# Second layer's cross-attention: float32 scores of 16 rows in TensorE's four row groups, in place of stacked bf16 parts

## The chip, the cores and the metric

The kernel runs on one core of a Trainium2 chip. The core has TensorE (matmuls), VectorE, ScalarE, GpSimd and queues for transfers. TensorE reads its operands from SBUF (128 partitions) and writes to PSUM, eight banks of 128 partitions x 512 float32. The metric is the device time of one execution in microseconds (us). The kernel before takes 3047.73 us (median of three runs, 3041.04 to 3049.35).

## What is computed

A decoder of two layers on x of shape (4, 512, 256): layer one has a state-space block, an attention with a feed-forward, a cross-attention and eight experts; layer two has an attention in blocks of 64, a cross-attention, and sixteen experts with a shared feed-forward. The change is in layer two's cross-attention alone:

```python
def _L1_xattn_ref(Q, K, V, Wq, bq, Wk, bk, Wv, bv, We, be):
    B, L, D = Q.shape            # 4, 512, 256
    H, E = 16, D // 16           # 16 heads of 16
    q = (Q @ Wq + bq).reshape(B, L, H, E)
    k = (K @ Wk + bk).reshape(B, S, H, E)
    v = (V @ Wv + bv).reshape(B, S, H, E)
    scores = jnp.einsum('blhe,bshe->bhls', q, k)
    A = jax.nn.softmax(scale * scores, axis=-1)      # scale = 1/4
    out = jnp.einsum('bhls,bshd->blhd', A, v).reshape(B, L, H * E)
    return out @ We + be
x = x + _L1_xattn_ref(_layernorm(x), ctx, ctx, ...)
```

## The kernel before

Each engine has one program, written out by hand, and they meet at semaphores. `Sig` names a semaphore with its count per sample. `Lane` is a ring of PSUM banks: `fill` makes TensorE wait until the tile that had the bank is drained, `take` makes the reader wait until the tile is full. In layer two `LBA` (banks 0, 1) is drained by ScalarE and `LBV` (banks 2, 3) by VectorE. `LBM` is one bank (1) for ten tiles of the softmax ("md": rows of maxima `MT_AT`, flips `FL_AT`, flips back `OTB_AT`), `LBO` one bank (0) for the weighted sums.

Layer two runs sample by sample (`for b in range(B)`, four samples). Activations have features on partitions and 512 positions along the free axis. One sample is, in TensorE's order:

1. Rotary query and key tiles (`rope_pair`), values (`v2_`), then the cross-attention's keys (`yk`, two tiles, drained by ScalarE to `kf`). Query and key rows of the block attention are rearranged by 16 transfers on SP's queue (L580).
2. The block attention (`block_scores`, `transpose_weights`, `weigh_blocks`), with the shared feed-forward of the sample before put in between (`ffn_gate`, `ffn_out`; none in sample 0). VectorE masks, finds maxima and sums, and in between splits `kf` into three bf16 parts (`split_step`, five steps, L2215 casts and L2217 subtractions).
3. The output projection (`wo`), whose sum with x VectorE makes; then the layer norm: mean (`norm_mean`), `centre` on VectorE, squares on ScalarE, `norm_var`, root, reciprocal, `norm_rows`, `norm_apply`. Between these stand the key stacks (`stack`, L1168): for each head three bf16 matmuls with 0/1 matrices (`sel_k`) put the parts, in the order `K_ORDER`, on 128 partitions, and ScalarE (L1723) drains them to `k_stack`. A product of two stacks is the sum of eight products of parts, near float32.
4. Queries (`yq`) from the normed x, values (`yv`); VectorE adds the bias, scales by 0.25 (L2257) and splits the queries (five steps); then sixteen query stacks.
5. Scores for the maxima (`scores_for_max(u)`, L1208): 64 tiles of 128 queries x 512 keys, one bf16 matmul each; VectorE takes the negated maximum of every row (`row_max`, L2272). The first sixteen use banks 4 to 7, later ones banks 2 and 3. Per group of four heads VectorE splits the maxima in three bf16 parts (`split_max`, L2285, L2287), TensorE turns them to rows (`rows_of_max`, L1216), VectorE casts these (`take_rows`, L2293).
6. The loop over 32 steps v (`scores_less_max(v)`): two heads and 128 keys to a step, transposed scores of 512 queries in banks 4+5 or 6+7, two bf16 matmuls (L1227) and two of 3 rows that add the negated maximum (L1230). ScalarE takes the exponential of both banks at once (L1750). Every second step `weigh_heads` (L1240) multiplies with values and a column of ones for four heads, in four column groups of 32. In step v TensorE issues the scores of step v + 1 first, then the maxima of a later group (`MAX_PER`, two or three a step), then a flip, rows or weighing if due.
7. Flips of the sums, division, flip back, the projection `we`, and the norms for the next sample and for the experts.

After four samples come the router and the sixteen experts, which the change does not touch. While layer one's experts run, VectorE sets up the selection matrices, and ScalarE's queue loads layer two's weights (`w1_loads`).

Of the kernel before, what the change touches and what calls it, by code (L numbers as in the profile page):

```python
# [7 lines left out]
P = 128  # L8
# [14 lines left out]
Q_ORDER, K_ORDER = (0, 0, 1, 1, 0, 2, 1, 2), (0, 1, 0, 1, 2, 0, 2, 1)  # L23
SR = len(Q_ORDER) * LE


# [10 lines left out]
MAX_PER = [3, 3] + [2] * 19  # L37
KS_PARTS = (0, 4, 8, 12, 14, 16)
# [33 lines left out]
class Lane:  # L72
# [22 lines left out]
    def take(self, eng, rnd, group, i):  # L95

        j = self.upto(group, i)
        eng.wait_ge(self.full.sem, self.full.at(j + 1, rnd))
        return self.banks[j % len(self.banks)]


def decoder_program(nc, A, out):
# [5 lines left out]
    with ctx:  # L108
# [127 lines left out]
        w_yq, w_yk, w_yv, w_ye, b_yv = take(KD, D), take(KD, D), take(KD, D), take(KD, D), take(D)  # L236
# [4 lines left out]
        sel_q, sel_k = [[take16(8, SR) for _ in range(3)] for _ in range(2)]  # L241
# [31 lines left out]
        kf, k_parts = take(KD, L), [take16(KD, L) for _ in range(3)]  # L273
        v1o = take(NC * LH * 2 * LE).rearrange("p (c h e) -> p c h e", c=NC, h=LH)
        pr1 = [take(2, L) for _ in range(4)]
        xnn1 = pr1[0].rearrange("p a b -> p (a b)").rearrange("p (c n) -> p c n", c=NC)
        negm1, nm_parts, nm_rows = take(NC, LH), take16(NC, P), [take16(L) for _ in range(2)]
        o_sb, rinv1 = [take(L) for _ in range(2)], take(NC, 4)
        nm_cols = nm_parts.rearrange("p c (h i) -> p c h i", i=32)
        outn, sd0, x_odd = take(NC, D), take(NC), take(KD, L)  # L280

        qf = take(KD, L, at=blocks_at)
        q_parts = [take16(KD, L, at=blocks_at + (2 + i) * L) for i in range(3)]
        xc0, sq0 = take(KD, L, at=blocks_at), take(KD, L, at=blocks_at + 2 * L)
        q_stack = take16(LH, L, at=turns_at)
        k_stack, oTb, o_all = take16(LH, L, at=scores_at), take(KD, L, at=scores_at + 8 * L), take(NC, D, at=scores_at + 10 * L)
# [101 lines left out]
        s1_full, s1_max, p1_ready = sig("s1_full", U1), sig("s1_max", U1), sig("p1_ready", V1)  # L388
        s2_full, pv1_done, o1_step = sig("s2_full", V1), sig("pv1_done", 4 * (NC - 1)), sig("o1_step", 8)
        kq_step, nm_step, sel_made = sig("kq_step", 10), sig("nm_step", 20), sig("sel_made")  # L390
        def rounds(*groups):
# [3 lines left out]
                   rounds(("v2_", 2), ("yk", 2), ("pair", 3 * NC), ("ks", LH), ("qs", LH), ("xn", 2)))  # L395
        LBV = Lane(LV.full.later(B), LV.drained.later(B), bank[2:4],
                   [("rope_a0", 2), ("rope_b0", 6)] + [(f"{name}{b + i}", tiles) for b in range(B) for name, i, tiles in (
                       ("wo", 0, 2), ("yq", 0, 2), ("yv", 0, 2), ("we", 0, 2), ("rope_a", 1, 2), ("logit", 0, 1), ("rope_b", 1, 6)) if b + i < B])
# [4 lines left out]
        LBM = Lane(sig("md_tile"), sig("md_drained"), bank[1:2], (("md", 10),))  # L403
# [32 lines left out]
        def _(sp):  # L436
# [139 lines left out]
            for b in range(B):  # L576
# [9 lines left out]
                if b + 1 < B:  # L586
                    sp.wait_ge(LBV.full.sem, LBV.full.at(LBV.upto(f"yv{b}", 2)))
                    load_ctx(b + 1)
# [15 lines left out]
        def _(pe):  # L604
# [389 lines left out]
            pe.wait_ge(sel_made.sem, 1)  # L994
# [79 lines left out]
            for b in range(B):  # L1074
# [13 lines left out]
                for m in range(KD):  # L1088
                    project(LBA, f"yk{b}", m, w_yk, ctxB)
                w(qk_here, 16 * 16)  # L1090
                act_has(f"v2_{b}", 2)

# [72 lines left out]
                def stack(group, h, select, parts):  # L1165
                    t = LBA.fill(pe, 0, group, h)
                    for j in range(3):
                        r = mm(t[0:SR], select[j][:, h % 8, :], parts[j][:, h // 8, :], start=j == 0, stop=j == 2)  # L1168
                    r.then_inc(LBA.full.sem, 1)

                def key_stacks(n):
                    for h in range(KS_PARTS[n], KS_PARTS[n + 1]):
                        stack(f"ks{b}", h, sel_k, k_parts)

                w(kq_step, 5)
                key_stacks(0)
# [10 lines left out]
                for m in range(KD):  # L1187
                    project(LBV, f"yq{b}", m, w_yq, xn)
# [8 lines left out]
                def scores_for_max(u):  # L1197
# [6 lines left out]
                    else:  # L1204
                        if u >= 4 * NC + 2:
                            w(s1_max, u - 1)
# [1473 lines left out]
```

## Time and profile before

| | |
|---|---|
| runs (us) | 3047.73, 3041.04, 3049.35 |
| profiled execution | 3043.07 us, span 3041.3 us |
| mean granted TensorE clock | 0.936 |
| TensorE matmul, share of the span | 2707.5 us, 89% |
| TensorE weight load | 1579.5 us, 52% |
| VectorE | 1508.0 us, 50% |
| ScalarE | 1149.9 us, 38% |
| reductions for the maxima (L2272), 256 | 163.0 us, 685 ns each |
| exponentials (L1750), 128 | 129.3 us, 1024 ns each |
| drains of the stacks (L1723), 128 | 75.9 us, 596 ns each |
| layer two's four samples | from about 1741 to 2580 us |

A row of windows gives its bounds and length, then the busy us (with the number of instructions) of TensorE, its weight loads, VectorE, ScalarE and GpSimd, then the granted TensorE clock (1.00 is 2.4 GHz, 0.50 is 1.2 GHz), the share of DMA and GB/s. Busy time of TensorE is modelled from the starts of its matmuls; neighbouring records overlap, so lengths are best read from one start to the next. A float32 matmul leaves two records, a bf16 one leaves one. In the timelines a line merges consecutive instructions of one line of the code; in square brackets stands the idle time of the engine before it and what ended it. "PE" is TensorE, "PEld" its weight loads, "DVE" VectorE, "ACT" ScalarE.

### The profile page before, as it was taken

What the parts mean: (1) busy time and instruction counts of PE and PEld (TensorE: products, weight loads), DVE (VectorE), ACT (ScalarE), POOL (GpSimd) and SP (SyncE); (2) the same over time, 40 slices, a digit from 0 to 9 for tenths busy, and PEclk for the clock granted to TensorE, in tenths of its full rate; (3) what the DMA queues carried; (4) which work ended last, traced back from release to release, by engine and by line L of the source; (5) the groups of instructions that cost most, each with busy time, mean ns of one, the idle gap of its engine ahead of it and who ended that gap; (6) DMA issues with size and microseconds to landing.
All of it is one profiled execution on the core that took longest, in us unless ns stands there. A gap on an engine that the chain in (4) does not pass through costs nothing. (4 is left out here: it accounts for less than half of the span.)

```text
span 3041.3 us, 40614 instructions
## 1 busy us (share of the span) xinstructions
PE 2707.5 (89%) x16481; PEld 1579.5 (52%) x16481; DVE 1508.0 (50%) x2382; ACT 1149.9 (38%) x1989; POOL 681.7 (22%) x364
## 2 busy tenths in 40 slices
PE   7779999999999999999869888988988998699997
PEld 4355534753285426653358653452542533487776
DVE  5565356833784277634611146346455554644442
ACT  4673245533472255424313225345344344011111
POOL 0254035801572065503320200000000000022222
PEclk9889999999999999999879879999899898699999
DMA  5540003100120003000179610100100101144443
GB/s 191 217 157 22 1 0 113 38 1 1 49 101 2 1 1 129 22 1 0 41 269 333 247 25 7 22 22 1 22 22 1 22 8 52 50 146 149 146 166 84
DMA packets 62130, 218.76 MB, mean 72 GB/s; under 512 B 12293, under 2 KB 28122, under 8 KB 45178
## 3 DMA queue, kind: packets, MB, share of 16 engines
q1 hardware_dynamic: 45802, 187.39, 17.1%
q0 software_dynamic: 9568, 18.75, 2.5%
q10 hardware_dynamic: 6576, 10.05, 0.9%
q8 instruction: 130, 2.13, 0.3%
q14 instruction: 54, 0.44, 0.0%
HBM read 171.98 MB, written 39.99 MB: 70 GB/s over the span
## 5 line engine op out<-in xcount | busy, mean ns | idle before, releaser
L610 PE MATMUL psum<-arena 128*128 128x256 f32 (+7 forms) x4160 | 1084.1, 412 | 67.7 <-ACT arena L1488 11.5
L610 PEld LDWEIGHTS psum<-arena 128*128 128x128 f32 (+1 forms) x4160 | 679.6, 200 | 423.9 <-issue 312.4
L2500 POOL TENSOR_TENSOR arena<-arena 128x1024 f32<-128x1024 f32 x128 | 299.9, 2370 | 110.2 <-DVE arena L1958 95.2
L1958 DVE TENSOR_TENSOR_SCAN arena<-arena,psum 128x512 f32<-128x512 f32 x256 | 291.5, 1201 | 26.1 <-PE psum L751 17.7
L751 PEld LDWEIGHTS psum<-arena 128*128 128x128 f32 x2048 | 242.9, 198 | 47.5 <-ACT arena L1518 40.3
L751 PE MATMUL psum<-arena 128*128 128x128 f32 x2048 | 253.5, 283 | 1.9 <-issue 1.9
L2535 POOL DMA_INDIRECT arena<-xn,arena x32 | 31.6, 987 | 959.8 <-DVE arena L2442 908.4
L2507 POOL TENSOR_TENSOR arena<-arena 128x1024 f32<-128x1024 f32 x32 | 75.9, 2373 | 656.8 <-ACT arena L1606 656.8
L2272 DVE TENSOR_REDUCE arena<-psum 128x1 f32<-128x512 f32 x256 | 163.0, 685 | 84.5 <-PE psum L1208 84.3
L2052 DVE SCALAR_TENSOR_TENSOR arena<-psum,arena 128x1024 f32<-128x1024 f32 x128 | 156.9, 1244 | 80.4 <-PE psum L896 80.1
L1606 ACT ACTIVATE arena<-arena 128x1024 f32<-128x1024 f32 x128 | 146.7, 1146 | 110.1 <-DVE arena L2052 109.9
L1750 ACT ACTIVATE arena<-psum 128x1024 f32<-128x1024 f32 x128 | 129.3, 1024 | 115.9 <-PE psum L1230 115.4
L1790 ACT ACTIVATE arena<-psum 128x256 f32<-128x256 f32 x128 | 49.2, 384 | 320.3 <-PE psum L610 320.3
L1511 ACT ACTIVATE arena<-arena 128x512 f32<-128x512 f32 x256 | 162.9, 708 | 0.0
L2511 POOL TENSOR_TENSOR arena<-arena 128x1024 f32<-128x1024 f32 x64 | 151.2, 2363 | 10.2 <-ACT arena L1606 1.3
L907 PE MATMUL psum<-arena 128*64 128x512 f32 x512 | 138.2, 617 | 15.5 <-ACT arena L1606 7.4
L896 PE MATMUL psum<-arena 64*128 64x512 f32 x512 | 142.5, 638 | 2.7 <-ACT arena L1584 2.7
L2036 DVE RECIPROCAL arena<-arena 128x256 f32<-128x256 f32 x64 | 110.9, 1743 | 46.1 <-ACT arena L1598 46.1
L1405 PE MATMUL psum<-arena 128*128 128x256 f32 x512 | 116.0, 378 | 0.0
L1518 ACT ACTIVATE arena<-arena 128x128 f32<-128x128 f32 x256 | 81.5, 390 | 82.4 <-PE psum L751 60.2
L2465 DVE TENSOR_TENSOR arena<-arena,psum 128x256 f32<-128x256 f32 x128 | 53.3, 421 | 116.3 <-ACT arena L1790 114.5
L1723 ACT ACTIVATE arena<-psum 128x512 bf16<-128x512 f32 x128 | 75.9, 596 | 80.7 <-PE psum L1168 78.1
(299 smaller groups left out, 3217.4 us busy)
## 6 DMA issues: line engine op xcount, KB each, us to landing
arena<-in_W SPq DMA_DIRECT2D x46, 1024.0 KB
arena<-c_rows SPq DMA_DIRECT2D x32, 512.0 KB, 3.8
arena<-in_Wg SPq DMA_DIRECT2D x16, 1024.0 KB, 4.9
arena<-in_Wu SPq DMA_DIRECT2D x16, 1024.0 KB, 7.6
arena<-in_Wd SPq DMA_DIRECT2D x16, 1024.0 KB, 10.0
arena<-in_xT SPq DMA_DIRECT2D x8, 512.0 KB, 5.4
zs_all<-arena SPq DMA_DIRECT2D x4, 1024.0 KB, 3.9
ut_all<-arena SPq DMA_DIRECT2D x4, 1024.0 KB, 8.7
```

The costliest lines, as they stand in the source:

```text
L610: r = mm(dst, w, x, start=i == 0, stop=i == len(pairs) - 1)
L751: r = mm(bank[4 + c][:, q * P:(q + 1) * P], duT[:, q, c * P:(c + 1) * P], diag[n % 2][:, q, :], start=True, stop=True)
L896: i = mm(bank[2 + 2 * (u % SBUFS) + r], xkT[64 * r:64 * r + 64, hp, kc * P:(kc + 1) * P], xqT[64 * r:64 * r + 64, hp, :], start=True, stop ...
L907: i = mm(bank[0][64 * r:64 * r + 64, :], v1[:, kc, 2 * hp + r, :], t2[u % TBUFS][:, r, :], start=kc == 0, stop=kc == NC - 1)
L1511: A_(dA[n % 2][:, c, :], dl[:, c, :], ACT.Exp, scale=aneg[:, c, n:n + 1]).then_inc(dA_ready.sem, 1)
L1606: A_(t2[u % TBUFS], rl[u % RBUFS], ACT.Square, scale=0.125, bias=vec[:, V_NB:V_NB + 1])\
L1750: A_(pr1[v % 4], psum[:, 4 + 2 * (v % 2):6 + 2 * (v % 2), :], ACT.Exp).then_inc(p1_ready.sem, 1)
L1958: V.tensor_tensor_scan(hs[n % 3][:, c, :], dA[n % 2][:, c, :], bank[4 + c], 0.0, ALU.mult, ALU.add)\
L2052: V.scalar_tensor_tensor(rl[u % RBUFS], t, minus_nb8, bound[:, kc, :].unsqueeze(1).broadcast_to([P, 2, L]), ALU.max, ALU.min).then_inc(rel ...
L2272: V.reduce_max(negm1[:, qc, h:h + 1], t, AX.X, negate=True).then_inc(s1_max.sem, 1)
L2500: nc.gpsimd.tensor_tensor(h, h, c_all[:, n % CBUFS, :].unsqueeze(1).broadcast_to([P, 2, L]), ALU.mult)\
L2511: nc.gpsimd.tensor_tensor(t, t, t2[kc], ALU.add).then_inc(tsum_step.sem, 1)
```

## The change

Queries and keys keep float32, and no parts or stacks are made. `_lay_out` pads each head of 16 columns of Wq and Wk (and of the biases) to 32 with zeros, so that the projections give four tiles of four heads, head j of a tile on partitions 32j to 32j + 15; partition 32j + 16 is 0 in the queries (until the negated maximum is added) and 1 in the keys (a bias of 1). Scores for the maxima are one float32 matmul of 16 rows, the scores of the loop one of 17 rows, in row group j. The order of the maxima is by group of four heads, block of queries, head; so four consecutive ones lie in four row groups. The negated maxima stand in columns 32j + 16 of `row_neg`, are transposed in float32, and added to the queries (`add_rows`). The scale of 0.25 goes to the exponential. `Placed` replaces the ring for the maxima after the first sixteen, their rows, flips and flips back: banks 1, 2, 3 in turn as long as there are maxima, then bank 1. 24 maxima instead of 20 are done ahead of the loop. Values are projected where the old keys were (ahead of the block attention), the keys' four tiles stand between the steps of the norm. The load of the next context waits for the keys instead of the values.

```diff
@@ constants
-Q_ORDER, K_ORDER = (0, 0, 1, 1, 0, 2, 1, 2), (0, 1, 0, 1, 2, 0, 2, 1)
-MT_AT, FL_AT, OTB_AT = (0, 1, 3, 6), (2, 4, 7, 8), (5, 9)
-MAX_AHEAD = 20
+MAX_AHEAD = 24
+def _cross_tiles():
+    order = [("max", 16), ("max", 17), ("row", 0)] + [("max", u) for u in range(18, MAX_AHEAD)]
+    for v in range(32):
+        order += [("max", u) for u in range(MAX_AHEAD + 2 * v, min(MAX_AHEAD + 2 * v + 2, 64))]
+        if v % 8 == 3 and v > 8:
+            order.append(("flip", v // 8 - 1))
+        if v % 8 == 5 and v < 24:
+            order.append(("row", v // 8 + 1))
+        if v == 22:
+            order.append(("back", 0))
+    return order + [("flip", 3), ("back", 1)]
+class Placed:
+    def fill(self, pe, rnd, tile):
+        n = self.number[tile]
+        before = [i for i in range(n) if self.places[i] == self.places[n]]
+        if before:
+            pe.wait_ge(self.drained.sem, self.drained.at(before[-1] + 1, rnd))
+        return self.banks[self.places[n]]
...
+        LBM = Placed(sig("md_tile"), sig("md_drained"), bank, cross,
+                     [1 + i % 3 if i <= cross.index(("max", U1 - 1)) else 1 for i in range(len(cross))])
@@ TensorE
                 norm_mean(x_b, 4)
-                key_stacks(1)
+                for g in range(2):
+                    project(LBA, f"yk{b}", g, w_yk, ctxB)
                 norm_var(mid_norm(b), sq, 5)
-                key_stacks(2)
+                project(LBA, f"yk{b}", 2, w_yk, ctxB)
                 norm_rows(mid_norm(b), sd, 4)
-                key_stacks(3)
+                project(LBA, f"yk{b}", 3, w_yk, ctxB)
                 w0(nb.out, mid_norm(b) + 1)
-                for m in range(KD):
-                    project(LBV, f"yq{b}", m, w_yq, xn)
...
+                for g in range(2):
+                    project(LBA, f"yq{b}", g, w_yq, xn)
 
                 def scores_for_max(u):
...
-                    mm(t, q_stack[0:SR, h, qc * P:(qc + 1) * P], k_stack[0:SR, h, :],
-                       start=True, stop=True).then_inc(s1_full.sem, 1)
+                    mm(t, q4[32 * j:32 * j + LE, g, qc * P:(qc + 1) * P], k4[32 * j:32 * j + LE, g, :],
+                       start=True, stop=True).then_inc((s1_full if u < LH else LBM.full).sem, 1)
...
                 def scores_less_max(v):
...
                     for j in (j0, j0 + 1):
-                        mm(bank[4 + 2 * (v % 2) + j % 2], k_stack[0:SR, 4 * g + j, kc * P:(kc + 1) * P],
-                           q_stack[0:SR, 4 * g + j, :], start=True, stop=False)
-                    for j in (j0, j0 + 1):
-                        r = mm(bank[4 + 2 * (v % 2) + j % 2], ones16[32 * j:32 * j + 3, :],
-                               nm_rows[g % 2][32 * j:32 * j + 3, :], start=False, stop=True)
+                        r = mm(bank[4 + 2 * (v % 2) + j % 2], k4[32 * j:32 * j + LE + 1, g, kc * P:(kc + 1) * P],
+                               q4[32 * j:32 * j + LE + 1, g, :], start=True, stop=True)
                     r.then_inc(s2_full.sem, 1)
...
+                for qc in range(NC):
+                    if qc == 0:
+                        act_has(f"yq{b}", 1)
+                    if qc >= 2:
+                        project(LBA, f"yq{b}", qc, w_yq, xn)
+                    for u in range(NC * qc, NC * (qc + 1)):
                         scores_for_max(u)
...
@@ ScalarE
+                def keys_in(g):
+                    t = LBA.take(act, 0, f"yk{b}", g)
+                    A_(k4[:, g, :], t, ACT.Identity, bias=vec[:, V_BK + g:V_BK + g + 1]).then_inc(LBA.drained.sem, 1)
@@ VectorE
-                    split_step(0, kf, k_parts, p)
...
+                def add_rows(g):
+                    t = LBM.take(dve, b, ("row", g))
+                    V.tensor_tensor(q4[:, g, :], q4[:, g, :], t, ALU.add).then_inc(LBM.drained.sem, 1)
```

## Rows read from the trace of the kernel before

**Rows 1.** Windows of sample 1: busy us per engine, clock, DMA share, GB/s.

```profile
2053.00:2068.00 15.00, 13.59 (x61) 5.13 (x58) 12.64 (x24) 7.81 (x14) 0.00 (x0) 1.00 0.00 1
2068.00:2137.00 69.00, 61.34 (x334) 16.27 (x334) 36.63 (x72) 35.82 (x37) 0.00 (x0) 0.98 0.00 1
```

**Rows 2.** Timeline of sample 1, output projection to maxima: start, length, engine, line.

```profile
2021.98 3.60 PE L610 MATMUL psum<-arena 128*128 128x512 f32 x8
...
2025.62 0.69 DVE L2173 TENSOR_TENSOR arena<-arena,psum 128x512 f32<-128x512 f32 x1 [1.03 <-PE psum L610]
...
2028.23 1.88 PE L610 MATMUL psum<-arena 128*128 128x512 f32 x4
...
2033.94 1.84 PE L610 MATMUL psum<-arena 128*128 128x1 f32 x16
...
2038.45 1.05 PE L1022 MATMUL psum<-arena 128*128 128x128 f32 x8
...
2040.82 7.17 PE L610 MATMUL psum<-arena 128*128 128x512 f32 x24
...
2052.90 1.03 PE L1208 MATMUL psum<-arena 128*128 128x512 bf16 x4
2053.31 2.48 DVE L2272 TENSOR_REDUCE arena<-psum 128x1 f32<-128x512 f32 x4 [2.10 <-PE psum L1208]
```

**Rows 3.** Timeline, layer one's cross-attention: matmuls in two row groups.

```profile
411.82 2.85 PE L896 MATMUL psum<-arena 64*128 64x512 f32 x12 [0.69 <-ACT arena L1584]
```

**Rows 4.** Timeline of sample 1, the loop: a weighing, its successors; exponentials 21 and 31.

```profile
2077.92 1.07 PE L1240 MATMUL psum<-arena 128*32 128x512 f32 x8
2078.92 0.61 PE L1227 MATMUL psum<-arena 128*128 128x512 bf16 x2
...
2081.87 1.07 PE L1240 MATMUL psum<-arena 128*32 128x512 f32 x8
...
2117.28 1.02 ACT L1750 ACTIVATE arena<-psum 128x1024 f32<-128x1024 f32 x1 [2.07 <-PE psum L1230]
...
2134.38 1.02 ACT L1750 ACTIVATE arena<-psum 128x1024 f32<-128x1024 f32 x1 [1.11 <-PE psum L1230]
```

**Rows 5.** Timeline: waits at the block attention, and ahead of layer one's experts.

```profile
1546.77 0.69 PE L967 MATMUL psum<-arena 128*128 128x128 f32 x2 [31.20 <-DMA arena<-slots_x]
...
1973.48 0.78 PEld L1101 LDWEIGHTS psum<-arena 16*64 16x64 f32 x64 [0.76 <-DMA arena<-arena]
...
1986.19 0.90 PE L1101 MATMUL psum<-arena 16*64 16x64 f32 x64 [0.91 <-issue]
```

**Rows 6.** Timeline of sample 1, from maximum 15 to the first exponential.

```profile
2064.91 0.20 DVE L2285 CAST arena<-arena 128x16 bf16<-128x16 f32 x1
...
2067.48 0.68 DVE L2293 CAST arena<-psum 128x512 bf16<-128x512 f32 x1
...
2068.22 0.61 PE L1227 MATMUL psum<-arena 128*128 128x512 bf16 x2 [0.21 <-DVE arena L2293]
...
2069.23 1.28 ACT L1750 ACT_TABLE_LOAD   x1 [3.44 <-PE psum L1230]
...
2070.53 3.07 ACT L1750 ACTIVATE arena<-psum 128x1024 f32<-128x1024 f32 x3
```

**Rows 7.** Windows around a fall of the clock (columns as rows 1), and exponentials there.

```profile
2084.30:2087.70 3.40, 1.86 (x15) 0.56 (x16) 2.06 (x4) 1.19 (x2) 0.00 (x0) 1.00 0.00 0
2087.70:2091.10 3.40, 3.40 (x13) 0.36 (x6) 0.98 (x2) 1.23 (x3) 0.00 (x0) 0.50 0.00 0
...
2087.07 1.02 ACT L1750 ACTIVATE arena<-psum 128x1024 f32<-128x1024 f32 x1 [2.21 <-PE psum L1230]
...
2090.86 1.02 ACT L1750 ACTIVATE arena<-psum 128x1024 f32<-128x1024 f32 x1 [0.90 <-PE psum L1230]
...
2106.54 1.02 ACT L1750 ACTIVATE arena<-psum 128x1024 f32<-128x1024 f32 x1 [2.21 <-PE psum L1230]
...
2108.94 1.02 ACT L1750 ACTIVATE arena<-psum 128x1024 f32<-128x1024 f32 x1 [0.24 <-PE psum L1230]
```

More of the change, by code:

```diff
@@ L99, in take, with __init__, upto @@
         return self.banks[j % len(self.banks)]
+class Placed:
+    def __init__(self, full, drained, banks, tiles, places):
+        self.full, self.drained, self.banks, self.places = full, drained, banks, places
+        self.number = {tile: n for n, tile in enumerate(tiles)}
+        self.full.per = self.drained.per = len(tiles)
+    def upto(self, tile):
+        return self.number[tile] + 1
+    def fill(self, pe, rnd, tile):
[4 more added lines that the diff above has]
+        return self.banks[self.places[n]]
+    def take(self, eng, rnd, tile):
+        eng.wait_ge(self.full.sem, self.full.at(self.upto(tile), rnd))
+        return self.banks[self.places[self.number[tile]]]
 def decoder_program(nc, A, out):
@@ L1087, in _ @@
                 pe.wait_ge(ld_cB.sem, ld_cB.at(16, b))
-                for m in range(KD):
-                    project(LBA, f"yk{b}", m, w_yk, ctxB)
+                for i in range(2):
+                    t = LBV.fill(pe, 0, f"yv{b}", i)
+                    for c in range(2):
+                        r = acc(t[:, c * D:(c + 1) * D],
+                                [(ctxB[:, k, (2 * i + c) * P:(2 * i + c + 1) * P], w_yv[:, k, :]) for k in range(KD)])
+                    r.then_inc(LBV.full.sem, 1)
                 w(qk_here, 16 * 16)
                 act_has(f"v2_{b}", 2)
+                dve_has(f"yv{b}", 2)
                 def block_scores(p):
@@ L1163, in _ @@
                     project(LBV, f"wo{b}", m, w_wo1, oT1)
[L1165 to L1176, printed above, removed]
                 dve_has(f"wo{b}", 2)
@@ L1222, in scores_less_max @@
                     if v % 8 == 0:
-                        w(LBM.drained, MT_AT[g] + 1)
+                        w(LBM.drained, LBM.upto(("row", g)))
                     if v >= 2:
@@ L1276, in _ @@
                 scores_less_max(0)
-                n_max = MAX_AHEAD
                 for v in range(V1):
@@ L1294, in _ @@
                     turn_y(b + 1)
+                w(LBM.drained, LBM.upto(("max", U1 - 1)))
                 tiles = [LBV.fill(pe, 0, f"we{b}", m) for m in range(KD)]
@@ L1300, in _ @@
                         flip_back(1)
-                    w(LBM.drained, OTB_AT[k] + 1)
+                    w(LBM.drained, LBM.upto(("back", k)))
                     for m in range(KD):
@@ L1687, in _ @@
                     r.then_inc(LBA.drained.sem, 1)
-                for m in range(KD):
-                    t = LBA.take(act, 0, f"yk{b}", m)
-                    A_(kf[:, m, :], t, ACT.Identity, bias=vec[:, V_BK + m:V_BK + m + 1]).then_inc(LBA.drained.sem, 1)
                 def drain_pair(p):
@@ L1740, in drain_o @@
                     if g >= 2:
-                        w(LBM.full, FL_AT[g - 2] + 1)
+                        w(LBM.full, LBM.upto(("flip", g - 2)))
                     A_(o_sb[g % 2], t, ACT.Identity).then_inc(LBO.drained.sem, 1)
@@ L2208, in pair_out @@
                     r.then_inc(bo_step.sem, 1)
-                def split_step(base, v, parts, i):
-                    if i > 0:
-                        w(kq_step, base + i)
-                    if i % 2 == 0:
-                        V.tensor_copy(parts[i // 2], v).then_inc(kq_step.sem, 1)
-                    else:
-                        V.tensor_tensor(v, v, parts[i // 2], ALU.subtract).then_inc(kq_step.sem, 1)
+                for i in range(2):
+                    t = LBV.take(dve, 0, f"yv{b}", i)
+                    V.tensor_tensor(v1o[:, 2 * i:2 * i + 2, :, 0:LE],
+                                    b_yv.rearrange("p (h e) -> p h e", h=LH).unsqueeze(1).broadcast_to([P, 2, LH, LE]),
+                                    t.rearrange("p (c h e) -> p c h e", c=2, h=LH), ALU.add).then_inc(LBV.drained.sem, 1)
                 def mask_scores(p):
```

198 lines of the change are left out of this document (63 added, 135 removed).

## The prediction

> **What bounds the kernel now.** I read the split by stage first (busy time of each engine in windows of the second sample; the four samples of layer two repeat within some tenths, except that sample 0 has no interleaved feed-forward work), then the timeline of that sample around the changed steps, then the clock. In the cross-attention no engine is full by the average, but TensorE comes nearest: 13.59 of 15 us and 61.34 of 69 us, against 36.63 us for VectorE and 35.82 us for ScalarE in the second of these stretches [rows 1]. So the reader should look for two things: chains in which TensorE waits for a conversion on another engine, and what a pair of steps costs on TensorE itself.
>
> The price list comes first. A float32 matmul leaves two records; eight records run from 2021.98 to where the next work starts at 2025.42, so a float32 matmul of 512 columns takes 0.86 us on the whole array [rows 2]. Used in row groups, six float32 matmuls of 64 rows (12 records) take 2.85 us: two at a time, 0.86 us per pair plus some 0.2 us at the ends [rows 3]. Four of 32 columns, side by side, take 1.00 us from their start to the next start (2077.92 to 2078.92) [rows 4]. No row shows four groups of 32 rows with 128 columns each. The bounds of such a quad are 0.86 us (all four together) and 1.72 us (two at a time); I take 0.96 us, since four tiles of the other kind do run together, 0.1 us being the exposed weight load and change of tiling.
>
> **Part 1, from the output projection to the first maximum.** Today: the projection ends at 2025.42, key stacks follow, and the mean of the norm starts at 2028.23 though its input is ready at 2026.31 (VectorE's second add at 2025.62, 0.69 long) [rows 2]. With the stacks gone the mean starts at 2026.4 and the squares are done at 2030.2. Now two key projections (3.44 us) stand behind the mean, 2028.1 to 2031.55, so the variance starts at 2031.55, not 2033.94. Its 1.7 us, the root and the reciprocal give 2034.2; the third key projection holds TensorE to 2035.0; then the factors' rows start at 2035.0, not 2038.45 [rows 2]. They need 2.37 us until the query projection starts (2038.45 to 2040.82), which gives 2037.4, and the fourth key projection holds TensorE until 2037.6. Gain 3.2 us. ScalarE's four key drains of 0.6 us lie beside this work; each is over before its bank is asked for again.
>
> Two of four query projections (3.44 us) end at 2041.0; the first one is drained meanwhile, and there are no bf16 parts to make. Maxima 0 to 3 start together, and VectorE starts 1.07 us later (0.86 for the matmul and 0.21 for the hand-over, which is the 0.41 us from 2052.90 to 2053.31 less the 0.2 us of a bf16 matmul, four of which start and end within 1.03 us): 2042.2 instead of 2053.31 [rows 2]. The gain is now 11.1 us: 3.2 from above, the rest is the chain of subtractions and casts on VectorE and the stacks behind it. The value projection moves ahead of the block attention in place of the old key projection, with the same TensorE time (3.44 us); its two VectorE adds delay nothing there, as the block attention's start waits for query and key rows by DMA (0.76 us at 1973.48), which gives them that time and more [rows 5].
>
> **Part 2, maxima 0 to 15.** VectorE needs 0.62 us for each (2.48 us for four) [rows 2], 9.9 us in all. The third query projection cannot start before matmul 7 is through the array; VectorE has run dry for 1.6 us when maximum 8 is ready, and for 0.3 us behind the fourth. Sum 11.9 us (2042.2 to 2054.1), where now it is 11.6 (2053.31 to 2064.91) [rows 2, 6]. Gain left: 10.8 us.
>
> **Part 3, to the first exponential.** Now 5.6 us (2064.91 to 2070.53) [rows 6]: split, two maxima, rows, cast, two maxima, scores, table load. After: transposes of the maxima 0.9 us, the add 0.7 us (like the cast, 0.68), then six maxima instead of two, in three banks, and then the scores: a bank comes free 0.74 us after its reader starts (2067.48 to 2068.22) [rows 6]. Step by step: maxima 18, 19, 20 start at 2055.2, 2055.5 and 2056.2, 21 to 23 follow their readers at 2057.1, 2057.7 and 2058.3, the scores behind them are full at 2059.5, the table load takes 1.28 us, and the exponential starts at 2060.9. That is 6.8 us; gain left 9.6 us. The four maxima done early are missing later.
>
> **Part 4, the loop.** Now a pair of steps takes 3.95 us (2077.92 to 2081.87) [rows 4]. After, TensorE's own work is less (two quads of 0.86 and 1.0 for the weighing, 2.7 us), but there is a wait in it: the second maximum of a step wants the bank of the first maximum of the step before. That one is read 1.07 us after its start and free 0.74 us later, 1.81 us; the second maximum starts there with its exposed weight load (0.96 us), and behind it stand the change of tiling and the weighing (1.1 us) and the next scores. 1.81 + 0.96 + 1.1 = 3.87, I take 3.95: no gain in a pair. Ten pairs are 39.5 us, two transposes of maxima and two flips 1.0 us each, start-up 0.8: 44.3 us from exponential 0 to 21, now 46.75 (2070.53 to 2117.28). From 21 to 31 there are no maxima; scores and weighing cost the same as now, but the last rows of maxima are float32 and the flip back comes in another place: 18.3 instead of 17.1 us (2117.28 to 2134.38) [rows 4, 6]. Net 1.2 us gained; 10.8 us a sample, 43 us in four.
>
> **Part 5, the rest.** VectorE's splitting of the keys leaves the block attention. One of its steps delays TensorE there, which sits idle 0.91 us before 1986.19 (the product for the feed-forward is behind a subtraction) [rows 5]: 0.9 us in three samples, 2.7 us. The other four lie beside ScalarE's exponentials or in VectorE's idle time. The selection tables' set-up before layer one's experts lies under a 31.20 us wait for a scatter: nothing [rows 5]. The wider weights add 0.5 MB in a stretch of some 190 us: nothing. The context's next load is issued earlier and waits for nothing new.
>
> **Part 6, the clock.** With one matmul in one row group per 0.62 us the burst of maxima is thin work. In the trace TensorE's granted clock is 1.00 (2.4 GHz) while it is dense, and falls to 0.50 (1.2 GHz) at 2087.7, after a stretch in which it was busy only 1.86 of 3.4 us [rows 7]. What such a stretch costs in the loop can be read: exponential 8 to 9 takes 3.79 us (2087.07 to 2090.86) and the same place eight steps later at full clock 2.40 (2106.54 to 2108.94) [rows 7]: 1.4 us lost in 3.4 us, 0.41 per us at half clock. After, I expect the clock low from some point between maxima 12 and 23 until the loop is dense again, and in about half the samples also once between the query projections: 13 us per sample at half clock, times 0.41, 5.3 us; 21 us in four.
>
> The Trainium skill speaks for less than that: "TensorE: Matmul & The Clock Gate", section "Why this matters for your kernels", ties a fall to idle gaps between bursts of matmuls, and a burst with one matmul always in flight has no such gap. By that rule part 6 is nothing, which is the first rival below; the trace has no dense stretch in one row group that could decide it. The same page, section "Part 3: Packing small matmuls", gives 3.07 times the throughput for four row tiles; a quad would by that take 1.12 us (an estimate from it and the 0.86 us), not 0.96, and the sum would be some 10 us higher.
>
> **Sum.** 43 + 3 - 21 = 25 us. The profiled execution took 3043.07 us (span 3041.3); 3043 - 25 = 3018. The median of the runs shown is 4.7 us above that execution, so I put the forecast at 3020.
>
> **Rivals.**
> (a) The clock stays up. For it: part of the engine is always streaming. Against: the fall at 2087.7 came with TensorE far from idle. Then 3043 - 46 = 2997 us.
> (b) The clock, once low, stays low through the loop: slower than before. A pair at half clock: the first maximum is read after 1.93, its bank free 0.74 later (2.7), the second maximum 1.8, weighing 2.0: 6.5 us instead of 3.95, 26 us in ten pairs; the pairs without maxima some 1.8 us more each, 9 us; and 3 us before the loop. 38 us against 10.8 gained: 27 us a sample, 3150 us. It decides from about 26 us at half clock in a sample (10.8 / 0.41). For it: at half clock a matmul in two of four groups leaves much of the array unused. Against: today the clock is low for 3.4 us at 2087.7 and comes back, 0.98 over the whole 69 us [rows 1, 7], and in (b)'s own pair TensorE streams nearly without a break.
> (c) The row groups do not overlap as the change wants (two at a time, or the two passes of each matmul in strict order). For it: only pairs are shown for 128 columns. Against: side-by-side columns overlap in fours [rows 4]. A quad of 1.72 us adds 1.7 us to a pair, some 18 us a sample: 3090 us.
> (d) The mechanism works but more is lost in places than I see: the waits for banks in the loop take 4.4 us a pair (the reader late, the change of tiling twice), 4.5 us a sample: 3038 us, and up to 3056.
>
> **Numbers.** Forecast (3004 to 3036) 0.50, (a) 0.20, (b) 0.09, (c) 0.06, (d) 0.15. The range reaches down past (a), whose quad may cost 0.86, and up to the end of (d): 2988 to 3056 holds 0.85. 0.3% is 9 us, about what a measurement of this kernel tells from no change: of the median 3047.7: faster is below 3038.6, the forecast, (a) and a quarter of (d), 0.74; within is the rest of (d), 0.11; slower are (b) and (c), 0.15.
>
> **What the profile will show.** Part 1: the first 128x1 reduction of a sample 11 us sooner behind the output projection. Quad: four pairs of records starting within some 0.05 us of each other. Part 2: two holes in VectorE's row of sixteen reductions, 1.6 and 0.3 us. Part 4: exponentials in pairs 3.9 to 4.0 us apart, TensorE waiting for the reduction in each. Part 6: granted clock below 1.00 in the stretch from the last query projection to the second pair of the loop. The prediction is wrong if the loop's pair is not near 3.95 us, or if the clock is low for less than 5 or more than 20 us in a sample.

## The result, and the profile after

The changed kernel takes 3117.57 us (median of four runs, 3087.97 to 3133.28), the kernel before on the same chip 3048.54 us: ratio 1.0219, 95% interval 1.0166 to 1.0273. It is slower by 2.2%, where 0.9% faster was forecast. The profiled execution took 3123.31 us (span 3121.5), 80 us more than the one of before.

The page first: its row of the granted TensorE clock in 40 slices, and four of its groups of instructions (busy us, mean ns of one, then idle time ahead of them and what ended it).

```profile
span 3121.5 us, 40190 instructions
PEclk9889999999999999999699765886987977799999
...
L1224 PE MATMUL psum<-arena 16*128 16x512 f32 x512 | 241.5, 953 | 3.1 <-DVE arena L2253 3.1
L1755 ACT ACTIVATE arena<-psum 128x1024 f32<-128x1024 f32 x128 | 128.3, 1023 | 208.6 <-PE psum L1246 208.6
L2256 DVE TENSOR_REDUCE arena<-psum 128x1 f32<-128x512 f32 x192 | 126.2, 688 | 152.9 <-PE psum L1224 152.8
L1246 PE MATMUL psum<-arena 17*128 17x512 f32 x512 | 189.9, 944 | 2.8 <-ACT arena L1755 2.8
```

L1224 are the maxima's scores, L1246 the loop's, L1755 the exponentials (unchanged: 1023 ns each), L2253 and L2256 the reductions. ScalarE and VectorE now wait for these matmuls, and a record of one lasts some 950 ns on average, although it streams 512 columns as every other. In the row of before the slices of layer two stand at 7 to 9 tenths; here they fall to 6 and 5. The mean clock of the execution is 0.888, before it was 0.936.

Where the 80 us arise, read at the same four marks of every sample in both traces: 7.4 us of them are there before sample 0's cross-attention, most of it code that the change leaves alone (the mark, the second add of sample 0, is at 1827.3 us here, at 1819.9 before, and between 1815.9 and 1824.7 us in the traces of the experiments below, on both sides of before; so I take it for the spread from one execution to another, which no run shows by itself). From the first to the last exponential the four samples lose 36.6, 20.8, 20.8 and 19.2 us, 97.3 in all. From sample 0's mark to its first exponential, and between the loops, 30.0 us are gained. Behind the last exponential 5.5 us are lost; that stretch is as it was, and takes 489 to 499 us in the traces. 7.4 + 97.3 - 30.0 + 5.5 = 80.2.

Sample 1 in stages (us; "add" is the second VectorE addition of the output projection, the mark of [rows 2]):

| stage | before | predicted | after |
|---|---|---|---|
| add to first reduction | 27.7 | 16.6 | 16.8 |
| sixteen reductions | 11.6 | 11.9 | 13.8 |
| to exponential 0 | 5.65 | 6.8 | 8.7 |
| exponential 0 to 21 | 46.75 | 44.3 | 67.9 |
| exponential 21 to 31 | 17.1 | 18.3 | 16.7 |

Windows of the changed kernel in sample 1, which answer to [rows 1] (bounds, length, busy us of TensorE, its weight loads, VectorE, ScalarE, GpSimd, granted clock, DMA share, GB/s):

```profile
2067.00:2081.00 14.00, 14.00 (x57) 7.19 (x55) 2.69 (x4) 6.80 (x10) 0.00 (x0) 1.00 0.12 37
2081.00:2085.00 4.00, 3.24 (x13) 1.47 (x10) 3.91 (x7) 0.00 (x0) 0.00 (x0) 1.00 0.00 0
2085.00:2088.40 3.40, 3.40 (x8) 1.09 (x10) 0.97 (x2) 0.31 (x1) 0.00 (x0) 0.52 0.00 0
2088.50:2095.30 6.80, 5.09 (x27) 1.92 (x21) 5.40 (x9) 0.97 (x2) 0.00 (x0) 1.00 0.01 2
2095.50:2103.50 8.00, 8.00 (x25) 5.13 (x24) 4.94 (x9) 1.20 (x1) 0.00 (x0) 0.50 0.00 0
2103.60:2153.30 49.70, 48.99 (x177) 14.90 (x180) 20.57 (x32) 15.85 (x16) 0.00 (x0) 0.50 0.00 0
2153.50:2160.10 6.60, 6.60 (x44) 1.91 (x40) 4.56 (x8) 4.48 (x5) 0.00 (x0) 1.00 0.01 2
2160.30:2170.40 10.10, 9.22 (x40) 2.81 (x34) 3.75 (x7) 2.05 (x2) 0.00 (x0) 0.50 0.00 0
2171.50:2188.20 16.70, 13.56 (x88) 3.96 (x88) 2.06 (x4) 10.40 (x12) 0.00 (x0) 1.00 0.00 1
```

The reader should see three things. The clock falls (1.00 to 0.52) right behind a stretch that holds only maxima, the matmuls of 16 rows at VectorE's pace, and comes back behind the full-array query projection that runs at 2084.7 to 2088.1. It falls again at 2095.4, and now stays at 0.50 (1.2 GHz) for 58 us, through the first seven pairs of the loop. And in that stretch TensorE is not idle: 48.99 of 49.70 us busy. Nor does a clock that has come back hold: it is at 1.00 for 6.6 us with TensorE busy throughout (2153.5 to 2160.1), and falls again. The 69 us of before stood at 0.98 [rows 1], with one stretch of 3.4 us at half clock and a return right after it [rows 7].

One pair of steps, first at half clock and then at full, in the timeline (start, length, engine, line, operation; L1256 is the weighing):

```profile
2132.07 1.02 ACT L1755 ACTIVATE arena<-psum 128x1024 f32<-128x1024 f32 x1 [1.39 <-PE psum L1246]
...
2133.78 1.02 ACT L1755 ACTIVATE arena<-psum 128x1024 f32<-128x1024 f32 x1 [0.69 <-PE psum L1246]
...
2138.84 1.02 ACT L1755 ACTIVATE arena<-psum 128x1024 f32<-128x1024 f32 x1 [4.04 <-PE psum L1246]
...
2154.04 1.94 ACT L1755 ACTIVATE arena<-psum 128x1024 f32<-128x1024 f32 x2 [4.62 <-PE psum L1246]
...
2156.88 0.70 PE L1246 MATMUL psum<-arena 17*128 17x512 f32 x2
2156.89 0.70 PE L1224 MATMUL psum<-arena 16*128 16x512 f32 x2
...
2157.86 0.59 PE L1246 MATMUL psum<-arena 17*128 17x512 f32 x2
2158.05 1.94 ACT L1755 ACTIVATE arena<-psum 128x1024 f32<-128x1024 f32 x2 [0.44 <-PE psum L1246]
```

A pair takes 6.77 us at half clock (2132.07 to 2138.84) and 4.01 us at full (2154.04 to 2158.05); before it took 3.95 [rows 4]. Two score matmuls and two maxima start within about 0.02 us of each other (2156.88, 2156.89), and the next scores start 0.98 us later (2157.86): the four row groups do work at the same time. So the change does on the array what it says, and the time is lost by the clock.

### The profile page after: what moved, and what is told of

It reads as the page before. It is cut to its first block and busy times, and to the rows that moved or that the text cites. A ratio compares the mean times of both kernels' runs of the same rounds, so it can differ in the third digit from the quotient of the medians.

```text
span 3121.5 us, 40190 instructions
## 1 busy us (share of the span) xinstructions
PE 2789.4 (89%) x16417; PEld 1618.8 (52%) x16417; DVE 1454.4 (47%) x2233; ACT 1090.8 (35%) x1885; POOL 682.2 (22%) x364
## 3 DMA queue, kind: packets, MB, share of 16 engines
q1 hardware_dynamic: 45802, 187.39, 16.8%
## 5 line engine op out<-in xcount | busy, mean ns | idle before, releaser
L642 PE MATMUL psum<-arena 128*128 128x256 f32 (+7 forms) x4224 | 1112.6, 415 | 68.1 <-ACT arena L1500 11.5
L642 PEld LDWEIGHTS psum<-arena 128*128 128x128 f32 (+1 forms) x4224 | 688.6, 199 | 440.6 <-issue 323.7
L1224 PE MATMUL psum<-arena 16*128 16x512 f32 x512 | 241.5, 953 | 3.1 <-DVE arena L2253 3.1
L1755 ACT ACTIVATE arena<-psum 128x1024 f32<-128x1024 f32 x128 | 128.3, 1023 | 208.6 <-PE psum L1246 208.6
L2256 DVE TENSOR_REDUCE arena<-psum 128x1 f32<-128x512 f32 x192 | 126.2, 688 | 152.9 <-PE psum L1224 152.8
L1246 PE MATMUL psum<-arena 17*128 17x512 f32 x512 | 189.9, 944 | 2.8 <-ACT arena L1755 2.8
L2471 POOL TENSOR_TENSOR arena<-arena 128x1024 f32<-128x1024 f32 x64 | 151.3, 2364 | 10.2 <-ACT arena L1618 1.3
L1224 PEld LDWEIGHTS psum<-arena 16*128 16x128 f32 x512 | 86.2, 275 | 90.0 <-issue 42.7
```

The source lines that it names most:

```text
L642: r = mm(dst, w, x, start=i == 0, stop=i == len(pairs) - 1)
L1224: mm(t, q4[32 * j:32 * j + LE, g, qc * P:(qc + 1) * P], k4[32 * j:32 * j + LE, g, :], start=True, stop=True).then_inc((s1_full if u < LH e ...
L1246: r = mm(bank[4 + 2 * (v % 2) + j % 2], k4[32 * j:32 * j + LE + 1, g, kc * P:(kc + 1) * P], q4[32 * j:32 * j + LE + 1, g, :], start=True, ...
L2471: nc.gpsimd.tensor_tensor(t, t, t2[kc], ALU.add).then_inc(tsum_step.sem, 1)
```

## The experiments

Theory A: the clock follows how many rows of the array work, and matmuls of 16 and 17 rows, even four at once, leave it low once it has fallen. Nothing but the number of rows need then change to get it back. A 32-row slice of the same tiles can be taken without any other edit: the added rows hold zeros in the queries (or in both), so all results and all instructions stay as they are, and a matmul of 512 columns streams the same 512 columns. Rivals, by the letters of the expectations: B, rows don't matter, and the clock falls because TensorE waits for banks and readers; C, only the state at the loop's entry counts, since a clock that is up stays up; D, the effect is a step (in the run with 24 rows: a group counts only with all its 32 rows; in the run with 20: any count above 17 is enough); N, in the run with 20, that count still acts as 17. Without a letter: one of the two score steps alone is at fault.

**Both score steps with 32 rows.**

```diff
-mm(t, q4[32 * j:32 * j + LE, ...], k4[32 * j:32 * j + LE, ...])            # maxima
+mm(t, q4[32 * j:32 * j + 2 * LE, ...], k4[32 * j:32 * j + 2 * LE, ...])
-mm(..., k4[32 * j:32 * j + LE + 1, ...], q4[32 * j:32 * j + LE + 1, ...])  # loop
+mm(..., k4[32 * j:32 * j + 2 * LE, ...], q4[32 * j:32 * j + 2 * LE, ...])
```

> The changed kernel, with all score matmuls on the full 32 rows of their row group instead of 16 (maxima) or 17 (loop). The added rows hold zeros, so the sums and the number and length of the matmuls are the same; only the number of rows that take part doubles. Theory A (the clock answers to how many rows work, and with 16 or 17 of 128 it stays at 1.2 GHz through the loop): the clock may still fall in the thin burst of maxima, but comes back in the first pairs of the loop; pairs of exponentials go from 6.78 to about 4.0 us, 100 us less in all: 3010 to 3035 us, mean clock 0.92 or more. Rival B (the clock falls because TensorE waits for banks and readers; rows do not matter): nothing changes, 3090 to 3125 us, mean clock about 0.89.

Measured: 3004.10 us (2999.74 to 3011.02), before 3046.93, ratio 0.9865 (0.9844 to 0.9886). That is 1.4% faster than the kernel before, and just below the 3010 to 3035 us of theory A. The page, sample 1 in windows, and two pairs of the loop:

```profile
PEclk9889999999999999999969978999989998699999
...
L1224 PE MATMUL psum<-arena 32*128 32x512 f32 x512 | 176.2, 688 | 3.1 <-DVE arena L2253 3.1
L1246 PE MATMUL psum<-arena 32*128 32x512 f32 x512 | 124.7, 659 | 5.2 <-ACT arena L1755 5.2
```

```profile
2032.00:2045.70 13.70, 11.38 (x36) 4.14 (x36) 9.76 (x17) 1.37 (x2) 0.00 (x0) 0.88 0.00 1
2045.70:2054.40 8.70, 8.25 (x28) 5.54 (x28) 6.16 (x11) 1.30 (x2) 0.00 (x0) 0.61 0.00 0
2054.40:2098.00 43.60, 41.67 (x257) 13.01 (x257) 27.67 (x46) 21.59 (x23) 0.00 (x0) 1.00 0.00 1
2098.00:2114.80 16.80, 13.64 (x92) 4.04 (x88) 2.06 (x4) 10.42 (x12) 0.00 (x0) 1.00 0.00 1
```

```profile
2067.31 1.94 ACT L1755 ACTIVATE arena<-psum 128x1024 f32<-128x1024 f32 x2 [2.66 <-PE psum L1246]
...
2071.33 1.94 ACT L1755 ACTIVATE arena<-psum 128x1024 f32<-128x1024 f32 x2 [0.44 <-PE psum L1246]
...
2075.34 1.94 ACT L1755 ACTIVATE arena<-psum 128x1024 f32<-128x1024 f32 x2 [2.07 <-PE psum L1246]
```

In this sample the loop has clock 1.00 over its whole length, its pair takes 4.01 us, exponential 0 to 21 is 43.7 us instead of 67.9. Sample 0 has the same 43.7; samples 2 and 3 have 5.0 and 6.8 us at half clock in that stretch and take 45.5 and 46.9. The burst in front is still thin (0.88 and 0.61), and the loop is entered with the clock only just back, in sample 2 even at half clock: with 32 rows too the clock falls in the burst, but the loop recovers. The price can be read from the two kernels: a mean clock of 0.888 over 3121.5 us means 2 x 0.112 x 3121.5 = 699 us at half clock, 0.934 over 3001.8 us means 396 us. The spans differ by 119.7 us, the time at half clock by 303 us: 0.40 us lost for each. Read stage by stage, 286 of the 303 us and 113 of the 119.7 us lie between the adds and the last exponentials of the four samples. B falls, A holds.

**Only the loop, or only the maxima, with 32 rows.** One of the two edits above at a time.

> As the first, but only the loop's scores use 32 rows; the maxima keep 16. Theory A: part of the rows only, so the clock comes back in the loop later than with both, but earlier than in the changed kernel: 3030 to 3085 us. Rival B: 3090 to 3125 us.

> As the first, but only the matmuls for the maxima use 32 rows; the loop's scores keep 17. Theory A: as with the loop's scores alone while there are maxima, 3030 to 3085 us; without maxima (steps 20 to 31) a low clock may stay. Rival B: 3090 to 3125 us.

Measured: loop alone 3015.64 us, ratio 0.9900 (0.9880 to 0.9919); maxima alone 3011.56 us, ratio 0.9886 (0.9866 to 0.9906); mean clock 0.927 in both. Both are below the 3030 to 3085 us of theory A, which had expected less of one edit alone. Either edit is enough to get the loop back to full clock for most of its length: exponential 0 to 21 takes 47.4 us with the loop alone and 47.3 to 47.4 us in three of four samples with the maxima alone, some 3.7 us more than the 43.7 of two samples with both. Windows of sample 1 with the loop alone, from the last of the sixteen reductions on:

```profile
2050.50:2059.20 8.70, 8.62 (x28) 5.54 (x28) 5.70 (x11) 1.30 (x2) 0.00 (x0) 0.54 0.00 0
2059.20:2066.00 6.80, 6.09 (x31) 1.63 (x30) 2.79 (x5) 3.32 (x4) 0.00 (x0) 0.59 0.00 0
2066.00:2106.60 40.60, 39.73 (x232) 12.46 (x228) 25.31 (x42) 18.27 (x21) 0.00 (x0) 0.96 0.00 1
```

The clock is low in the first steps still (0.59, where both edits together had 1.00 from the first exponential on), and once more for a moment near step 20; in between it is up. B falls here too, and neither step is the fault alone. What decides is what the two put on the array together, as the next run bears out. That the maxima alone should do as well as the loop alone I had not expected so clearly.

**24 rows, then 20, in both steps.** The size of the suspected cause is varied: `32 * j + 24` and `32 * j + 20` as the end of all four slices.

> The changed kernel with 24 rows in every score matmul, zeros in the added ones. Theory A (the clock answers to how many rows work): a time between the changed kernel (3118) and 32 rows (3004), by the run with 32 rows in the loop only (3016) nearer to the latter: 3008 to 3045 us. Rival D (a step: either 32 rows of a group are used, or the group counts for nothing): as the changed kernel, 3090 us or more.

> The changed kernel with matmuls of 20 rows in both score steps (the added rows hold zeros). Theory A (the time at half clock follows from how many rows of the array work, so the loss shrinks row by row): 20 rows stand between 17 (3118 us, loop entered and left at half clock for some 50 us) and 24 (3016 us): the loop is at half clock in a part of its steps, exponentials 0 to 21 take 50 to 64 us, 3030 to 3095 us in all. Rival D (every count above 17 gives full clock, as a step): exponentials 0 to 21 in 44 to 48 us, 3008 to 3025 us. Rival N (20 rows still act as 17): 66 to 70 us, 3105 to 3130 us.

Measured: 24 rows 3016.45 us, ratio 0.9896 (0.9876 to 0.9916), mean clock 0.924, exponential 0 to 21 47.4 to 47.6 us in all four samples. These are the values of the two runs above, whose score matmuls have 24 and 24.5 rows on average: samples 1 and 2 of all three runs have 20.5 us at half clock from the add to exponential 31, where both steps with 32 rows have 10.2 and the changed kernel 71.7. 20 rows 3057.78 us (3042.56 to 3073.09), ratio 1.0048 (1.0023 to 1.0072), mean clock 0.910, and that stage takes 51.6, 63.9, 47.1 and 64.0 us. With 20 rows, windows of the loops of samples 0 to 3:

```profile
1861.00:1882.00 21.00, 20.49 (x83) 6.03 (x82) 8.85 (x14) 7.25 (x8) 0.00 (x0) 0.53 0.00 0
1882.00:1912.00 30.00, 29.12 (x178) 9.04 (x174) 19.56 (x33) 14.38 (x16) 0.00 (x0) 1.00 0.00 1
2063.00:2113.00 50.00, 49.29 (x181) 15.10 (x183) 20.49 (x32) 15.79 (x16) 0.00 (x0) 0.50 0.00 0
2113.00:2127.00 14.00, 13.12 (x82) 3.95 (x76) 8.41 (x14) 6.54 (x8) 0.00 (x0) 1.00 0.01 1
2282.00:2328.00 46.00, 44.43 (x252) 13.75 (x256) 27.74 (x46) 21.23 (x23) 0.00 (x0) 0.91 0.00 1
2480.00:2529.00 49.00, 48.74 (x180) 14.94 (x183) 19.74 (x31) 15.03 (x16) 0.00 (x0) 0.50 0.00 1
```

The same instructions spend about 20 (2 x 0.47 x 21.00), 50, 8 (2 x 0.09 x 46.00) and 49 us at half clock in four samples of one execution: 20 rows is a size at which the loop may or may not come back at once, and its runs spread by 30 us. So the loss grows as rows are taken away (3004, 3016, 3058, 3118 us with 32, 24, 20 and 16/17 rows). D falls in both forms, and N with it; both medians lie in the ranges of A, though one sample with 20 rows (47.1 us) is as fast as D would have it.

**Full-array matmuls ahead of the loop.** To tell C from A the loop must be entered at full clock with 16/17 rows: twelve float32 matmuls of 128 rows into a free bank, their results unused, ahead of the first scores of the loop. The control has the same twelve and 32 rows.

```diff
+for _ in range(12):
+    mm(bank[0], ident, k4[:, 0, :], start=True, stop=True)
 scores_less_max(0)
```

> The changed kernel (16 and 17 rows) with twelve more float32 matmuls of the whole array (512 columns, 10.3 us at full clock, identity times keys into a bank that nobody reads) between the last maximum ahead of the loop and the loop's first scores. The loop is thus entered at 2.4 GHz, with no change of its own instructions. Theory A (the loop's own rows bring the clock down and keep it there): exponentials 0 to 21 still take 60 us or more where the kernel with 32 rows takes 43.7, in all 3140 to 3175 us. Rival C (the loop only inherits the low clock from the burst, and holds a high one): exponentials 0 to 21 take 44 to 46 us, in all 3050 to 3085 us.

> The same twelve matmuls in the kernel with 32 rows, as the control: the block costs 10.3 us at full clock and some 2 us more for what begins at half clock, less the few us that are low before the loop now: 8 to 12 us a sample, 3036 to 3055 us. Exponentials 0 to 21 take 43.7 us in every sample by both theories.

Measured: 3163.51 us, ratio 1.0379 (1.0349 to 1.0409) with 16/17 rows; 3065.78 us, ratio 1.0065 (1.0044 to 1.0087) with 32. Sample 1 in windows, first the kernel with 16/17 rows, then the one with 32:

```profile
2105.00:2111.00 6.00, 5.49 (x21) 1.99 (x19) 0.48 (x1) 1.28 (x1) 0.00 (x0) 1.00 0.00 0
2111.00:2114.00 3.00, 1.91 (x16) 0.47 (x16) 1.50 (x4) 2.67 (x4) 0.00 (x0) 0.95 0.00 0
2114.50:2151.00 36.50, 36.50 (x136) 11.48 (x136) 14.82 (x24) 10.83 (x11) 0.00 (x0) 0.50 0.00 0
2151.00:2161.00 10.00, 10.00 (x66) 3.23 (x62) 6.05 (x10) 4.82 (x6) 0.00 (x0) 0.99 0.01 2
```

```profile
2075.00:2081.20 6.20, 5.66 (x21) 2.02 (x19) 0.51 (x1) 1.29 (x2) 0.00 (x0) 1.00 0.00 0
2083.60:2086.80 3.20, 3.20 (x16) 0.87 (x11) 1.17 (x2) 0.86 (x1) 0.00 (x0) 0.50 0.00 0
2087.00:2121.00 34.00, 34.00 (x211) 10.74 (x207) 22.40 (x36) 16.70 (x18) 0.00 (x0) 1.00 0.00 1
```

Both loops begin at clock 1.00. Both have a thin start, in which TensorE waits for ScalarE's first exponentials (1.91 of 3.00 us busy with 16/17 rows), and both fall behind it. With 32 rows the clock is back after some 3.4 us and holds for 37 us (one more stretch of 3.4 us comes just ahead of exponential 21); with 16/17 rows it is at 0.50 for more than 36 us in which TensorE is busy 36.50 of 36.50 us. It then holds 1.00 for 17 us (2151.2 to 2168.3) and falls again inside the loop. Exponentials 0 to 21 take 60.6, 60.8, 68.7 and 69.8 us, and the total is within the 3140 to 3175 us of A. So the entry doesn't decide, and C falls. The control cost more than I had expected (3065.78, not 3036 to 3055): the twelve matmuls delay the first exponential by 10 to 13 us a sample, and in three samples two stretches of 3.4 us at half clock make the loop 47.0 us instead of 43.7.

**A dense filler inside the burst of maxima** (run ahead of the two kernels above; it missed its aim). Behind every maximum from the fifth on, one bf16 matmul of 128 rows into a free bank, with 32 rows in the score steps, and again with 16/17.

```diff
 scores_for_max(u)
+if 4 <= u < MAX_AHEAD:
+    mm(bank[3 if u < LH else 0], ident16, ident16.unsqueeze(1).broadcast_to([P, 4, P]), start=True, stop=True)
```

> 32 rows everywhere, and behind each of the maxima 4 to 23 one more bf16 matmul of the whole array (128 rows, 512 columns, the identity), into a bank that nobody reads; it is extra work. Theory A: the array is no longer thin in the burst, the clock stays at 2.4 GHz from the query projections to the loop in most samples; the sixteen reductions take 12.2 instead of 13.8 us, the stretch to the first exponential 7 to 8 instead of 8.7: 2990 to 3001 us. Rival: the added matmuls and changes of tiling (0.3 us each) cost as much as the clock gives, or the clock falls all the same: 3004 to 3020 us.

> The changed kernel (16 and 17 rows) with the same added matmuls behind the maxima 4 to 23. The sample thus enters the loop at 2.4 GHz. Theory A: the loop's own scores leave too many rows idle; the clock falls in the loop within some steps and stays low: 3075 to 3115 us. Rival C (the loop only inherits the low clock from the burst and would hold a high one): 2995 to 3030 us.

Measured: 3135.45 us, ratio 1.0277 (1.0245 to 1.0309), and 3258.23 us, ratio 1.0689 (1.0614 to 1.0764). Both far off what was expected. The timeline of the first (L1227 is the filler) shows why:

```profile
1841.56 1.12 PE L1224 MATMUL psum<-arena 32*128 32x512 f32 x2 [0.77 <-DVE arena L2256]
...
1842.62 0.39 PE L1227 MATMUL psum<-arena 128*128 128x512 bf16 x1
...
1842.94 1.12 PE L1224 MATMUL psum<-arena 32*128 32x512 f32 x2
...
1844.31 1.12 PE L1224 MATMUL psum<-arena 32*128 32x512 f32 x2
```

A matmul of the whole array between two row groups keeps them from overlapping: a maximum with its filler takes 1.37 us (1842.94 to 1844.31) where VectorE needs 0.62, and the sixteen reductions take 24.4 to 30.6 us instead of 13.8. The filler slowed the burst instead of filling it. The run with 16/17 rows says nothing on C, since its loop was entered at half clock, against its expectation (in every sample 68.7 us for exponential 0 to 21, 61.9 of them low, and 27.2 for the rest, all low); therefore the twelve matmuls above.

**Fewer maxima ahead, with 32 rows.** `MAX_AHEAD = 20` instead of 24, the value of before.

> 32 rows everywhere, and 20 maxima ahead of the loop instead of 24. Reading of the trace: four maxima less ahead of the first exponential save 2.5 to 3 us a sample (0.62 to 0.75 each), and two more steps pairs with maxima cost 0.75 us each (4.01 against 3.25): net 1 to 1.5 us a sample, 2997 to 3002 us. Rival: the loop's maxima then hold up the rows of maxima (their last one is taken just before), and the two cancel: 3003 to 3010 us.

Measured: 3007.20 us (2999.85 to 3013.42), ratio 0.9864 (0.9841 to 0.9888), against 0.9865 with 24. The first exponential comes 5.3 us behind the sixteenth reduction, in one sample 4.7, instead of 8.7, and the four maxima are paid again behind it: 2.2 us between exponentials 21 and 31 (18.9 instead of 16.7), and the rest in the loop and the burst. It cancels, as the rival of that expectation had it (3003 to 3010 us).

**What no run measured.** The converse, the kernel before with fewer rows in its stacked matmuls and all else equal, has no measurement. The cause rests on rows added to the changed kernel, not on rows taken from the kernel before.

## Why the prediction was wrong

**The step that failed is Part 6**, the length of the stretch at half clock: 13 us per sample, "until the loop is dense again". From the add to exponential 31 the four samples of the changed kernel have 115.3, 71.7, 71.7 and 71.7 us at half clock, 83 on average (before 3.4, 3.4, 3.4 and 6.8). So both of the prediction's own signs of being wrong came: a clock low for more than 20 us in a sample, and a pair of 6.77 us instead of 3.95 in most of the loop. What came is rival (b), to which I gave 0.09. The price per us was right: 0.41 predicted, 0.40 measured between the kernels with 16/17 and with 32 rows. The length was wrong: 303 us more at half clock than with 32 rows in the whole execution. By the forecast's own price that is 303 x 0.41 = 124 us, where the two profiled executions differ by 119.7.

The rest of the sum erred on the other side, by less. The kernel with 32 rows has 7 to 17 us at half clock in that part of a sample, 11 on average, close to the 13 of Part 6; it takes 3004 us, at the lower end of the forecast's own range (3004 to 3036). Its profiled execution is 39.5 us faster than the one of before, where the sum says 25; most of the difference is in the loop (10.3 us gained instead of 4.8) and between the loops (8.5 instead of 2.7).

The mistake of reasoning: I took TensorE's busy time for density. The argument against (b) was that "in (b)'s own pair TensorE streams nearly without a break". It does, 48.99 of 49.70 us, and the clock stays at 0.50. The argument for (b), "at half clock a matmul in two of four groups leaves much of the array unused", was the right one, and I didn't follow it: 17 of 32 rows in each group leave nearly half of the array unused even when all four groups run. The trace of before could not show it, since its loop had scores of 128 rows; what it showed, a return within 3.4 us [rows 7], I carried over to a loop of other matmuls. No row there stood for a long stretch of thin matmuls, and such a term should have had wider ends.

The rule of the Trainium skill, "TensorE: Matmul & The Clock Gate", section "Why this matters for your kernels", which ties a fall to idle gaps between bursts, stood behind rival (a). This case's trace doesn't agree: the clock falls at 2160.2 behind 6.60 us without any idle time, and it is at 0.50 for 49.70 us with TensorE idle for 0.71 of them. The measurement decides.

The other steps:
- **Part 1** held: 16.8 us from the add to the first reduction, 16.6 predicted. The gain of 11 us is there (27.7 us before).

```profile
2064.27 0.69 DVE L2173 TENSOR_TENSOR arena<-arena,psum 128x512 f32<-128x512 f32 x1 [1.03 <-PE psum L642]
...
2073.79 1.05 PE L1053 MATMUL psum<-arena 128*128 128x128 f32 x8
...
2081.09 4.88 DVE L2253 TENSOR_REDUCE arena<-psum 128x1 f32<-128x512 f32 x8 [4.99 <-PE psum L1224]
```

The factors' rows start 9.5 us behind the add (2064.27 to 2073.79), where 9.4 was worked out (2035.0 less 2025.62).
- **Part 2**: 11.9 us predicted, 12.1 in samples with the clock up (two of the kernel with 32 rows), 13.8 where it falls between the query projections. That fall, foreseen for half of the samples, comes in all four of the changed kernel (15.2 us in sample 0) and in two of four with 32 rows.
- **Part 3**: 6.8 us at full clock predicted, 8.7 measured at clock 0.50 to 0.53. No run with these instructions had it at full clock throughout, so the 6.8 itself isn't shown; the shortest is 7.7 us, in sample 2 with 32 rows.
- **Part 4**: the quad of 0.96 us is 0.98 (2156.88 to 2157.86). The 1.12 us estimated from the Trainium skill's figure ("TensorE: Matmul & The Clock Gate", "Part 3: Packing small matmuls") is not borne out. The pair of 3.95 us is 4.01 at full clock; exponential 0 to 21 at full clock, with 32 rows, is 43.7 us where 44.3 was predicted. Exponential 21 to 31 was wrong in sign, though small: 16.7 us instead of 18.3 (17.1 before). Rivals (c) and (d) didn't come.
- **Part 5**: from exponential 31 of sample 0 to the add of sample 1 it is 95.9 us (before 97.0): 1.1 gained, 0.9 predicted. But the next two such stretches gain 4.3 and 3.6, 9.0 us in three where 2.7 was predicted. They have 35 us at half clock where before had 55. At 0.40 per us (an estimate, as that price is of the loop) this makes 8 of the 9 us and leaves 1 for the cause that Part 5 names; the forecast had no term for the clock here.
- **Rival (b)** itself was close in its pair (6.5 worked out, 6.77 measured) but too dear as a whole (3150 us): the clock came back for 6.8 us in the eighth pair, and in samples 1 to 3 for the last ten exponentials (16.7 us, where sample 0, at half clock from 1859.9 to 1972.5, needs 27.2).

What stays open: why the clock returned in the eighth pair of samples 1 to 3 and again for their last ten exponentials, whose scores have 17 rows too, while sample 0 stayed low; and why with 20 rows it was back early in one sample and late in others. No run tried it.

## What to carry to other kernels

Small contractions packed into TensorE's row groups should use all 32 rows of a group, zeros included: at full clock the pair takes 4.01 us either way, and here it turned 2.2% slower into 1.4% faster. When a change makes matmuls thinner, look at how much of the array they fill and not at TensorE's busy share, and price the case that a clock which has fallen doesn't come back. And don't put a matmul of the whole array between matmuls that should overlap in row groups.

## What the runs showed of the hardware

- TensorE's granted clock stays at 1.2 GHz for 58 us on end (in 49.70 us of them the engine is busy for 48.99), if the score matmuls use 16 or 17 rows of each group of 32; with 32 rows, the added ones adding zeros alone, it is at 2.4 GHz over the same work (43.6 us) in two of four samples, and has 5.0 and 6.8 us at 1.2 GHz in the others. So rows in use count even where their products are zeros.
- Either of two interleaved kinds of matmul brought to 32 rows is enough for most of that (3015.64 and 3011.56 us, against 3004.10 with both), as are 24 rows in both (3016.45 us).
- Four float32 matmuls of 512 columns in four row groups take 0.98 us at 2.4 GHz, one on the whole array 0.86 us [rows 2].
- A matmul of the whole array between two in single row groups costs their overlap: 1.37 us for a maximum and the filler together, at clock 1.00.
